# Masking the key-major probabilities of a fused two-layer network on GpSimd instead of adding the mask on TensorE

## The chip, the cores and the metric

The kernel runs on one core of one Trainium2 chip. The metric is the device time of one execution in microseconds (us). Below, PE is TensorE, DVE is VectorE, ACT is ScalarE, POOL is GpSimd and SP is SyncE, which here only issues DMAs.

## What is computed

Sixteen sequences of 512 tokens with 128 features go through two layers: a linear attention and a mixture of experts, then a causal softmax attention and a second mixture of experts. Only the second attention is touched:

```python
B, T, C = x.shape                                   # 16, 512, 128
q = jnp.einsum('btc,oc->bto', x, Wq).reshape(B, T, H, D)   # H 16, D 8
k = jnp.einsum('btc,oc->bto', x, Wk).reshape(B, T, H, D)
v = jnp.einsum('btc,oc->bto', x, Wv).reshape(B, T, H, D)
att = jnp.einsum('bqhd,bkhd->bhqk', q, k) * SCALE
att = jnp.where(mask[None, None, :, :], -jnp.inf, att)     # mask: key j > query i
att = jax.nn.softmax(att, axis=-1)
out = jnp.einsum('bhqk,bkhd->bqhd', att, v).reshape(B, T, C)
```

The mask hides every key behind its query, so of each head's 4 x 4 blocks of 128 the ones below the diagonal are whole, those above are left out by the kernel, and the four on the diagonal are half masked.

## The kernel before

**Stages.** Sequences are pipelined. Each round of the main loop has an x phase and a y phase. The x phase runs the ten expert networks of one sequence on PE, and beside them the scores of another sequence in query-major order, whose row maxima DVE takes (`maxima`). The y phase runs the same scores again in key-major order, 16 heads in 8 pairs, five banks ("fills") a pair, 40 fills a sequence. ACT takes the exponential of each filled bank into `probs` (`exps`, L1014), PE multiplies `probs` by the values (`outputs`, L835), four heads at a time. Beside this, the y phase runs the first attention of a later sequence (`f_...` steps) and the projections q and k of the next one (`r_...` steps). The main loop holds 13 rounds; what comes before and after it is written out.

**Banks and buffers.** Key-major fills go round three PSUM banks `ba0` to `ba2`, so PE may start fill n once ACT has finished fill n-3. `probs` holds three pairs: ACT may write pair p once PE has multiplied pair p-3.

**The mask.** In key-major order the first 128 columns of each head's block of 128 keys are the diagonal block. After each score product (L576) PE adds `mask_k`, zero or -1.0e38, with a second matmul (L578, `identb` as weights): 64 in each sequence, 1024 in all. The query-major scores have their own mask (`mask_q`, L583).

**The chain from q and k to the next x phase.** DVE adds the experts' output to x (L1371), computes the norm (`b_ve`, L1380), centres (`b_n`, L1149), adds a bias to the first attention's projections (`f_bias`, L1180), normalises them (`f_l2` and `f_scale`: 18 small operations at L1193 to L1195 on `rt`, `rn`, and two at L1202), and between them takes the rests of q and k (`qkr`, L1388, once for each). POOL splits each rest in two more parts (`qkp`, L486 and L488). SP writes the parts to device memory (L316), waits until they have landed, and then reads them back in another layout into `QT` and `KT` (L333): 18 transfers for the first eight heads, issued once 20 fills of this y phase are done, and 18 for the others, once all 40 are. The x phase of the next round needs them.

**POOL** also takes reciprocal roots (`power`, L452) and, in the x phase, the products with the gates (`gated`, L459). Its order in the y phase is `power` for `b_rs`, the two splits, `power` for `f_rs`, and the end of the loop.

**The end of a round** is a branch on each engine (L276 on DVE, ACT, PE and POOL). DVE's last work of the y phase are the gates of the experts and the last normalisation (L1404); its first of the x phase is a maximum (L1270).

Of the kernel before, what the change touches and what calls it, by code (L numbers as in the profile page):

```python
# [15 lines left out]
ALU = mybir.AluOpType  # L16
# [3 lines left out]
P = 128  # L20
BATCH, SEQ, D = 16, 512, 128
Q = SEQ // P
TOK = BATCH * SEQ
TILES = TOK // P
HEADS, HD = 16, 8
# [9 lines left out]
MASKED = -1.0e38  # L35
# [10 lines left out]
def build_kernel(nc, a, out):  # L46
    ctx = ExitStack()
    with ctx:
        def sb(name, shape, dt=F32):
            return ctx.enter_context(nc.sbuf_tensor(name, shape, dt))  # L50
# [27 lines left out]
        mask_k = sb("mask_k", [P, P], BF16)  # L78
# [108 lines left out]
        def sb3(name, shape, dt=F32):  # L187
# [56 lines left out]
            s_nmT s_mx0 s_mx1 s_st s_exp s_pv s_oT s_tr s_norm s_aTt s_aT s_wo s_x3 s_y s_ysq s_row s_T4 s_nT4 s_l1 s_l1c  # L244
# [7 lines left out]
        def apart(eng):  # L252

            eng.nop(nofuse=True)
# [164 lines left out]
        def _(pool):  # L419
            c = [1]  # L420

            def const(ins):

                c[0] += 1
                ins.then_inc(S["s_cst"], 1)
                pool.wait_ge(S["s_cst"], c[0])
# [8 lines left out]
            const(pool.memset(mask_k[:], 0.0))  # L435
            const(pool.affine_select(mask_k[:], mask_k[:], [[1, P]], ALU.is_ge, MASKED, base=0, channel_multiplier=-1))
# [40 lines left out]

            def y_phase(b, f, r, t):
                if r is not None:
                    power(b_rs[:], b_ve[:], "s_varb", "s_rsb", r + 1)  # L480
                if r is not None:
                    for w in range(2):

                        pool.wait_ge(S["s_r1"], 2 * r + w + 1)
                        apart(pool)
                        pool.tensor_copy(qkp[:, w, 1], qkr[:, w]).then_inc(S["s_p2"], 1)  # L486
                        pool.wait_ge(S["s_p2"], 2 * r + w + 1)
                        pool.tensor_tensor(qkp[:, w, 2], qkr[:, w], qkp[:, w, 1], ALU.subtract).then_inc(S["s_p3"], 1)  # L488
                if f is not None:
                    power(f_rs[:, 0:Q], f_ve[:, 0:Q], "s_varf", "s_rsf", 2 * f + 2)  # L490
# [67 lines left out]
        def scores(pe, b, n, by_key):  # L558
# [14 lines left out]
            for head, blk, col in groups:  # L573
                if by_key:
                    w = SEQ - blk * P
                    pe.matmul(bank[:, col:col + w], lhsT=KT[0:K_ROWS, head, blk * P:(blk + 1) * P],  # L576
                              rhs=QT[0:K_ROWS, head, blk * P:], start=True, stop=False)
                    last = pe.matmul(bank[:, col:col + P], lhsT=identb[:], rhs=mask_k[:], start=False, stop=True)  # L578
# [19 lines left out]
        def _(pe):  # L598
# [212 lines left out]
            def y_phase(b, f, r, t):  # L811
# [14 lines left out]
                def outputs(k):  # L826
                    pe.wait_ge(S["s_exp"], FILLS * b + 10 * k + 10)
# [820 lines left out]
```

## Time and profile before

| | us |
|---|---|
| median of three runs | 2169.51 |
| lowest and highest | 2169.4, 2172.93 |
| the execution that was profiled | 2157.45 |
| its span, first to last instruction | 2155.7 |

In the profiled span PE is busy for 1617.6 us (75%), DVE 1274.6 (59%), ACT 807.2 (37%) and POOL 510.8 (24%). One round of the main loop takes about 105 us; the loop and the sequences before and after it take up the first 1760 us or so, and the expert lists and the second mixture of experts the rest. Busy shares are means over such stages. The way to read this profile is to take one round, to find in it the waits that end last, and to ask which of them the edited work feeds.

### The profile page before, as it was taken

The page shows a single profiled execution, that of the slowest core. Times are in us where ns is not written, and L with a number is a line of the kernel's source. Part 1 is how long each engine was busy: PE and PEld are TensorE (multiplying, and loading weights), DVE is VectorE, ACT ScalarE, POOL GpSimd, SP SyncE. Part 2 cuts the span into 40 slices and gives each one's busy share as a digit, 9 for nine tenths or more (in the row PEclk, how much of TensorE's full clock was granted, in tenths as well). Part 3 has the DMA queues.
Part 4 walks back from the last instruction along what each step waited for, and adds up shares of the span by engine and source line. Part 5 has one row for each costly group of instructions (what it writes and reads, how often), then busy time and mean ns, then how long its engine had stood idle before and what let it go on. Part 6 is the DMA issues. An engine that isn't in the chain of part 4 may idle for free.

```text
span 2155.7 us, 35078 instructions
## 1 busy us (share of the span) xinstructions
PE 1617.6 (75%) x10136; PEld 908.6 (42%) x10136; DVE 1274.6 (59%) x3878; ACT 807.2 (37%) x1562; POOL 510.8 (24%) x481
## 2 busy tenths in 40 slices
PE   3779888887979797979797979797998831166771
PEld 2345444444444444444444444343544421145551
DVE  5456857575858484848485757576773547721113
ACT  1225252525344443434343435252534322323322
POOL 2321212121202121212121212112120020038884
PEclk7879998999999898989898999998998665588886
DMA  5032240304040403040404031313123000025457
GB/s 143 21 44 42 25 61 10 63 7 68 4 69 7 64 7 64 14 56 15 55 22 48 25 46 30 41 33 38 35 31 56 17 6 0 0 59 99 88 88 170
DMA packets 121515, 95.40 MB, mean 44 GB/s; under 512 B 13120, under 2 KB 115904, under 8 KB 121408
## 3 DMA queue, kind: packets, MB, share of 16 engines
q1 hardware_dynamic: 110144, 85.29, 22.3%
q0 software_dynamic: 11264, 9.05, 3.4%
q14 instruction: 85, 0.70, 0.2%
q8 instruction: 22, 0.36, 0.1%
HBM read 63.34 MB, written 30.18 MB: 43 GB/s over the span
## 4 chain that ended last, share of the span: by engine, by line
PE 38%; issue 26%; DVE 15%; POOL 6%; DMA 6%; ACT 3%; SPq 2%; DVEq 1%; POOLq 0%; ACTq 0%
PE bo L835 5%; PE ba L576 5%; PE fa L665 4%; PE ba L581 4%; PE fa L681 4%; POOL sum_rows L543 3%; PE facc L691 3%; SPq L333 2%; PE ba L578 2%; PE ba L583 2%; DMA xin<-in_L_attn_x 1%; DMA KT<-qk_parts 1%; POOL got L520 1%; DMA sum_rows<-contrib,cur 1%; DVE nm L1270 1%
## 5 line engine op out<-in xcount | busy, mean ns | idle before, releaser
L581 PE MATMUL ba<-KT,QT 72*128 72x512 bf16 (+3 forms) x1024 | 263.2, 320 | 181.1 <-DVE nm L1270 128.5
L1014 ACT ACTIVATE probs<-ba 128x512 f32<-128x512 f32 x640 | 330.2, 622 | 114.1 <-PE ba L578 113.4
L459 POOL TENSOR_TENSOR hh<-th,gb 128x512 f32<-128x512 f32 x128 | 162.1, 1267 | 706.6 <-ACT gb L967 432.7
L1270 DVE TENSOR_REDUCE nm<-ba 128x1 f32<-128x512 f32 x256 | 174.1, 680 | 182.5 <-issue 134.3
L576 PE MATMUL ba<-QT,KT 75*128 75x512 bf16 (+3 forms) x1024 | 252.6, 310 | 34.8 <-ACT probs L1014 28.8
L581 PEld LDWEIGHTS ba<-KT,QT 72*128 72x128 bf16 x1024 | 104.9, 102 | 343.8 <-DVE nm L1270 153.2
L583 PE MATMUL ba<-mask_q,identb 128*128 128x128 bf16 x1024 | 201.3, 230 | 0.0
L578 PE MATMUL ba<-mask_k,identb 128*128 128x128 bf16 x1024 | 195.7, 224 | 0.0
L665 PE MATMUL fa<-f_nT,w 128*128 128x512 f32 x320 | 186.8, 667 | 2.4 <-ACT sc L1048 1.2
L681 PE MATMUL fa<-f_nT,w 128*128 128x512 f32 x320 | 180.0, 645 | 0.0
L983 ACT ACTIVATE sil<-fa 128x512 f32<-128x512 f32 x160 | 95.1, 594 | 217.1 <-PE fa L665 217.0
L967 ACT ACTIVATE gb<-fa 128x512 f32<-128x512 f32 x128 | 76.3, 596 | 256.6 <-PE fa L673 256.5
L691 PE MATMUL facc<-hh,w 128*128 128x512 f32 x320 | 166.2, 602 | 0.0
L576 PEld LDWEIGHTS ba<-QT,KT 75*128 75x128 bf16 x1024 | 102.0, 100 | 148.7 <-ACT probs L1014 93.2
L835 PE MATMUL bo<-probs,vp 128*32 128x512 f32 (+3 forms) x2048 | 154.5, 443 | 0.8 <-DVE ao L1404 0.8
L1272 DVE TENSOR_REDUCE nm<-ba 128x1 f32<-128x384 f32 x256 | 139.9, 546 | 23.2 <-PE ba L583 23.1
L583 PEld LDWEIGHTS ba<-mask_q,identb 128*128 128x128 bf16 x1024 | 106.1, 104 | 82.4 <-issue 80.1
L452 POOL TENSOR_TENSOR b_rs<-b_ve,mhalf 128x4 f32<-128x4 f32 x48 | 48.5, 1010 | 334.3 <-DVE b_ve L1380 227.5
L1395 DVE COPY oT<-bo 128x512 f32<-128x512 f32 x64 | 44.1, 690 | 115.7 <-PE bo L835 114.7
L543 POOL DMA_INDIRECT sum_rows<-contrib,cur x64 | 100.7, 1573 | 30.8 <-issue 18.6
L578 PEld LDWEIGHTS ba<-mask_k,identb 128*128 128x128 bf16 x1024 | 102.8, 100 | 4.6 <-issue 3.7
L835 PEld LDWEIGHTS bo<-probs,vp 128*32 128x32 f32 x2048 | 60.5, 111 | 99.6 <-issue 72.6
(283 smaller groups left out, 2731.7 us busy)
## 6 DMA issues: line engine op xcount, KB each, us to landing
QT<-qk_parts SPq DMA_DIRECT2D x288, 64.0 KB
KT<-qk_parts SPq DMA_DIRECT2D x288, 64.0 KB
qk_parts<-qkp SPq DMA_DIRECT2D x32, 384.0 KB, 2.5
fc<-in_L_ffn_fc_weight SPq DMA_DIRECT2D x32, 256.0 KB, 3.2
xn_rows<-row SPq DMA_DIRECT2D x16, 288.0 KB, 2.5
sum_rows<-zrow SPq DMA_DIRECT2D x1, 4224.0 KB, 22.0
sums<-sum_rows SPq DMA_DIRECT2D x4, 1056.0 KB, 10.4
xin<-in_L_attn_x SPq DMA_DIRECT2D x16, 256.0 KB, 14.0
```

The lines of the kernel that those rows point to most:

```text
L459: pool.tensor_tensor(hh[:, e % 2], th[:, e % 2], gb[:, e % 2], ALU.mult).then_inc(S["s_h"], 1)
L543: pool.indirect_dma_start(sum_rows, bass.IndirectOffsetOnAxis(cur[k][:, c:c + 1], 0), contrib[k % 2][:, c], None, compute_op=ALU.add).then ...
L576: pe.matmul(bank[:, col:col + w], lhsT=KT[0:K_ROWS, head, blk * P:(blk + 1) * P], rhs=QT[0:K_ROWS, head, blk * P:], start=True, stop=False)
L578: last = pe.matmul(bank[:, col:col + P], lhsT=identb[:], rhs=mask_k[:], start=False, stop=True)
L581: pe.matmul(bank[:, col:col + w], lhsT=QT[0:QK_ROWS, head, blk * P:(blk + 1) * P], rhs=KT[0:QK_ROWS, head, 0:w], start=True, stop=False)
L583: last = pe.matmul(bank[:, col + w - P:col + w], lhsT=identb[:], rhs=mask_q[:], start=False, stop=True)
L665: pe.matmul(fa[0][:], lhsT=w1[:, e], rhs=f_nT[:], start=True, stop=True).then_inc(S["s_h1"], 1)
L681: pe.matmul(fa[1][:], lhsT=w3[:, e], rhs=f_nT[:], start=True, stop=True).then_inc(S["s_h3"], 1)
L691: pe.matmul(facc[:], lhsT=w2[:, e], rhs=hh[:, e % 2], start=e == 0, stop=e == U0 - 1).then_inc(S["s_ym"], 1)
L835: last = pe.matmul(bo[32 * j:32 * j + 32, blk * P:], lhsT=vp[:, blk, 4 * k + j], rhs=prob_block(4 * k + j, blk), start=blk == 0, stop=blk ...
L1014: act.activation(probs[:, pair % 3, f_], ba[n % 3][:], ACT.Exp, scale=SCALE).then_inc(S["s_exp"], 1)
L1270: last = dve.tensor_reduce(nm[:, 3, h:h + 1], bank[:], X, ALU.max, negate=True)
```

## The change

The matmul with `mask_k` after each key-major score product goes, with the constant itself. A new function `cut` on POOL waits for each exponential and writes zeros over the masked triangle of its diagonal blocks in `probs`, in place: one `affine_select` a fill, over one block (fills 0 and 2 of a pair) or over two blocks at once (fills 1, 3 and 4). `outputs` on PE waits for the new semaphore `s_cut` instead of `s_exp`. POOL's y phase is written in a new order around the cuts.

```diff
+            def cut(b, pair):
+
+                for f_ in range(5):
+                    pool.wait_ge(S["s_exp"], FILLS * b + 5 * pair + f_ + 1)
+                    apart(pool)
+                    row_ = probs[:, pair % 3, f_]
+                    if f_ in (0, 2):
+                        block_ = row_[:, 0:P]
+                        pool.affine_select(block_, block_, [[1, P]], ALU.is_ge, 0.0, base=0, channel_multiplier=-1).then_inc(S["s_cut"], 1)
+                    else:
+                        apart_by = 384 if f_ < 4 else 256
+                        blocks = row_.rearrange("p (n k) -> p n k", k=P)[:, 0:apart_by // P + 1:apart_by // P]
+                        pool.affine_select(blocks, blocks, [[0, 2], [1, P]], ALU.is_ge, 0.0, base=0, channel_multiplier=-1).then_inc(S["s_cut"], 1)
+
             def y_phase(b, f, r, t):
                 if r is not None:
                     power(b_rs[:], b_ve[:], "s_varb", "s_rsb", r + 1)
-                if r is not None:
-                    for w in range(2):
-
+                for pair in range(HEADS // 2):
+                    if b is not None:
+                        cut(b, pair)
+                    if r is not None and pair in (1, 2):
+                        w = pair - 1
                         pool.wait_ge(S["s_r1"], 2 * r + w + 1)
                         apart(pool)
                         pool.tensor_copy(qkp[:, w, 1], qkr[:, w]).then_inc(S["s_p2"], 1)
                         pool.wait_ge(S["s_p2"], 2 * r + w + 1)
                         pool.tensor_tensor(qkp[:, w, 2], qkr[:, w], qkp[:, w, 1], ALU.subtract).then_inc(S["s_p3"], 1)
-                if f is not None:
-                    power(f_rs[:, 0:Q], f_ve[:, 0:Q], "s_varf", "s_rsf", 2 * f + 2)
+                    if f is not None and pair == 4:
+                        power(f_rs[:, 0:Q], f_ve[:, 0:Q], "s_varf", "s_rsf", 2 * f + 2)
...
-                    pe.matmul(bank[:, col:col + w], lhsT=KT[0:K_ROWS, head, blk * P:(blk + 1) * P],
-                              rhs=QT[0:K_ROWS, head, blk * P:], start=True, stop=False)
-                    last = pe.matmul(bank[:, col:col + P], lhsT=identb[:], rhs=mask_k[:], start=False, stop=True)
+                    last = pe.matmul(bank[:, col:col + w], lhsT=KT[0:K_ROWS, head, blk * P:(blk + 1) * P],
+                                     rhs=QT[0:K_ROWS, head, blk * P:], start=True, stop=True)
...
-                    pe.wait_ge(S["s_exp"], FILLS * b + 10 * k + 10)
+                    pe.wait_ge(S["s_cut"], FILLS * b + 10 * k + 10)
```

POOL in the loop's y phase, before, from the root for `b_rs` to the end of the round (ISA and REGISTER_ALU rows are register work; the semaphores in brackets are those an instruction waits for):

```order
L452 TENSOR_TENSOR b_rs<-b_ve,mhalf 128x4 [waits s_varb]
L484 ISA
L486 CAST qkp<-qkr 128x512 [waits s_r1]
L488 TENSOR_TENSOR qkp<-qkr,qkp 128x512 [waits s_p2]
...
L452 TENSOR_TENSOR f_rs<-f_ve,mhalf 128x4 [waits s_varf]
L276 REGISTER_ALU
L276 COMPARE_AND_BRANCH
```

POOL at the same root for `f_rs`, after: the end of pair 4's cuts, the root, and the beginning of pair 5's:

```order
L487 AFFINE_SELECT probs<-probs 128x2x128 [waits s_exp]
L448 REGISTER_ALU
L449 TENSOR_TENSOR f_rs<-f_ve,mhalf 128x4 [waits s_varf]
L478 REGISTER_ALU
L483 AFFINE_SELECT probs<-probs 128x128 [waits s_exp]
```

So 25 cuts now stand ahead of this root in POOL's order and 15 behind it, and the 15 can't begin before it has run. The splits likewise stand behind the cuts of pairs 1 and 2.

PE before the third `outputs` of the y phase (heads 8 to 11), before:

```order
L576 MATMUL ba<-QT,KT 128x384 [waits s_exp]
L578 MATMUL ba<-mask_k,identb 128x128
L576 MATMUL ba<-QT,KT 128x128
...
L576 MATMUL ba<-QT,KT 128x256 [waits s_exp]
...
L835 MATMUL bo<-probs,vp 32x512 [waits s_norm,s_exp]
L835 MATMUL bo<-probs,vp 32x512 x3
```

PE at the same place, after:

```order
L589 MATMUL ba<-QT,KT 128x384 [waits s_exp]
L589 MATMUL ba<-QT,KT 128x128
L589 MATMUL ba<-QT,KT 128x256 [waits s_exp]
L589 MATMUL ba<-QT,KT 128x256
L847 MATMUL bo<-probs,vp 32x512 [waits s_norm,s_cut]
L847 MATMUL bo<-probs,vp 32x512 x3
```

Every second matmul of the key-major scores is gone, and the first product of each `outputs` now waits for POOL. This third one needs the cuts of pairs 4 and 5, and pair 5's are the first behind the root.

## Rows read from the trace of the kernel before

**Rows 1.** The page: span, and busy time of PE and POOL.

```profile
span 2155.7 us, 35078 instructions
PE 1617.6 (75%) x10136; PEld 908.6 (42%) x10136; DVE 1274.6 (59%) x3878; ACT 807.2 (37%) x1562; POOL 510.8 (24%) x481
```

**Rows 2.** Waits: who waited for whom, total us, times, longest.

```profile
DVE nm L1270 <- issue: 134.3, 12, 12.4
```

**Rows 3.** Chain that ended last, 950 to 1070: start, us, what.

```profile
1021.27 0.66 PE bo L842 x4
...
1048.40 11.01 issue
```

**Rows 4.** Timeline of SP's DMA issues, one round: start, us, line.

```profile
1017.54 5.66 SPq L316 DMA_DIRECT2D qk_parts<-qkp  x2
1025.61 0.32 SPq L333 DMA_DIRECT2D QT<-qk_parts  x1
...
1040.16 0.28 SPq L333 DMA_DIRECT2D QT<-qk_parts  x1
...
1048.72 0.67 SPq L333 DMA_DIRECT2D KT<-qk_parts  x1
```

**Rows 5.** Stretches: us, busy of the five engines, PEclk, DMA share, GB/s.

```profile
1053.00:1059.00 6.00, 0.00 (x0) 0.00 (x0) 0.00 (x0) 0.22 (x1) 0.00 (x0) 0.72 0.59 79
1059.00:1062.00 3.00, 1.73 (x6) 1.05 (x7) 2.48 (x6) 0.00 (x0) 0.00 (x0) 0.50 0.49 80
1062.00:1066.00 4.00, 4.00 (x11) 1.52 (x9) 2.02 (x5) 1.08 (x2) 1.26 (x1) 0.51 0.02 4
```

**Rows 6.** Timeline of DVE in the same round: start, us, line, operation.

```profile
1004.39 0.69 DVE L1371 TENSOR_TENSOR x<-facc,x 128x512 f32 x1 [1.43 <-PE facc L808]
...
1008.26 1.12 DVE L1149 TENSOR_SCALAR b_n<-x,b_mv,b_rs 128x128 f32 x4
...
1014.34 0.40 DVE L1195 SCALAR_TENSOR_TENSOR rn<-rt,rn 128x64 f32<-128x64 f32 x2
...
1016.27 1.27 DVE L1195 SCALAR_TENSOR_TENSOR rn<-rt,rn 128x64 f32<-128x64 f32 x2
...
1018.73 1.29 DVE L1202 TENSOR_TENSOR kvq<-kvq,rn 128x512 f32<-128x512 f32 x2
1019.93 0.68 DVE L1388 TENSOR_TENSOR qkr<-facc,qkp 128x512 f32<-128x512 f32 x1
```

**Rows 7.** Timeline of POOL in the same round.

```profile
1007.22 1.01 POOL L452 TENSOR_TENSOR b_rs<-b_ve,mhalf 128x4 f32<-128x4 f32 x1 [14.73 <-DVE b_ve L1380]
...
1016.16 1.16 POOL L488 TENSOR_TENSOR qkp<-qkr,qkp 128x512 bf16<-128x512 f32 x1
...
1033.92 1.01 POOL L452 TENSOR_TENSOR f_rs<-f_ve,mhalf 128x4 f32<-128x4 f32 x1 [11.31 <-DVE f_ve L1216]
```

**Rows 8.** Groups of POOL instructions by form: count, busy us, mean ns.

```profile
L439 POOL TENSOR_SCALAR_AFFINE_SELECT pick<-pick 128x1024 bf16<-128x1024 bf16 x3 | 3.3, 1091 | 0.4
L436 POOL TENSOR_SCALAR_AFFINE_SELECT mask_k<-mask_k 128x128 bf16<-128x128 bf16 x1 | 0.3, 292 | 0.1
```

**Rows 9.** Timeline of PE: a mask, the product behind it, and the third outputs.

```profile
1024.05 0.22 PE L578 MATMUL ba<-mask_k,identb 128*128 128x128 bf16 x1
1024.11 0.33 PE L576 MATMUL ba<-QT,KT 75*128 75x384 bf16 x1
...
1033.97 2.36 PE L835 MATMUL bo<-probs,vp 128*32 128x512 f32 x32
```

**Rows 10.** Timeline of ACT: exponentials of pairs 0 (three of five), 1, 5 with 6, and 7.

```profile
1006.54 1.57 ACT L1014 ACTIVATE probs<-ba 128x512 f32<-128x512 f32 x3 [0.50 <-PE ba L578]
...
1011.57 2.54 ACT L1014 ACTIVATE probs<-ba 128x512 f32<-128x512 f32 x5
...
1029.94 5.01 ACT L1014 ACTIVATE probs<-ba 128x512 f32<-128x512 f32 x10 [2.70 <-PE ba L578]
...
1038.30 2.55 ACT L1014 ACTIVATE probs<-ba 128x512 f32<-128x512 f32 x5
```

More of the change, by code:

```diff
@@ L77, in build_kernel @@
         mask_q = sb("mask_q", [P, P], BF16)
-        mask_k = sb("mask_k", [P, P], BF16)
         pick = sb("pick", [P, E0, P], BF16)
@@ L243, in build_kernel @@
             s_pad s_lnb s_varb s_rsb s_T3 s_nT3 s_q s_k s_v s_p1 s_r1 s_p2 s_p3 s_vp s_qkw s_qk0 s_qk1 s_S s_red s_nmp s_nmt
-            s_nmT s_mx0 s_mx1 s_st s_exp s_pv s_oT s_tr s_norm s_aTt s_aT s_wo s_x3 s_y s_ysq s_row s_T4 s_nT4 s_l1 s_l1c
+            s_nmT s_mx0 s_mx1 s_st s_exp s_cut s_pv s_oT s_tr s_norm s_aTt s_aT s_wo s_x3 s_y s_ysq s_row s_T4 s_nT4 s_l1 s_l1c
             s_l1x s_ex1 s_prob s_rowd s_mstep s_zero
@@ L434, in _ @@
             const(pool.affine_select(mask_q[:], mask_q[:], [[-1, P]], ALU.is_ge, MASKED, base=0, channel_multiplier=1))
-            const(pool.memset(mask_k[:], 0.0))
-            const(pool.affine_select(mask_k[:], mask_k[:], [[1, P]], ALU.is_ge, MASKED, base=0, channel_multiplier=-1))
             const(pool.memset(pick[:], 0.0))
```

## The prediction

> **What bounds the kernel now.** The page shows PE busy for 75% of the span [rows 1]. That would make any matmul taken out look like a gain, so I read next what ends the waits inside one round of the loop.
>
> The list of waits has one odd entry: DVE sits for 134.3 us in 12 waits in front of its first maximum of the x phase, 11.2 us each, and no engine or DMA is named for them, only "issue" [rows 2]. The loop has 13 rounds and returns 12 times, so this is what a return to the loop's head costs. The chain of waits has the same piece: 11.01 us from 1048.40 [rows 3]. Meanwhile PE, DVE and POOL do nothing at all, and the DMA engines stay at a share near 0.59 until about 1061.5; then their share falls to 0.02 [rows 5]. I read this as DVE's instructions at the loop's head being fetched by DMA, behind the queue of QT and KT transfers. The Trainium skill says, in "Runtime: NRT & Kernel Launch", section "Instruction fetch mechanics", that a taken branch out of the window of pages at hand must fetch the page by DMA before going on; the rows agree in kind, and the length (11 us) is this case's own.
>
> So one round is tied to its transfers. SP issues the first of the 36 at 1025.61 and the last at 1048.72 [rows 4], and they drain at about 1061.5, some 36 us after the first. The first waits for q and k to be split and written: the second rest starts on DVE at 1019.93 [rows 6], 5.7 us before it. And that rest is reached by a DVE chain of 15.5 us from 1004.39 (the experts' output added) which has hardly an idle moment [rows 6]. **The y phase's first half is DVE's, its end is hidden behind a DMA queue, and PE's load is in neither.** At the chain's end PE's turn of the first outputs starts at 1021.27, right behind DVE's work on the second rest and one copy of its outputs [rows 3, 6], so the rest of the y phase follows DVE too.
>
> **What is taken out.** A mask takes PE 0.06 us: one starts at 1024.05 and the next product at 1024.11 [rows 9] (the 0.22 us shown is the length of its pipeline). At 0.057 us, 64 masks are 3.6 us a sequence. ACT's ten exponentials back to back take 5.01 us [rows 10], so where ACT sets the pace the gain hides. Ahead of 1021 DVE sets it. What is left is PE's dense stretch from 1021 to 1030 and the first fills of some pairs, some 20 masks: 1.2 us, at the end of the y phase. Ends: 0 and 3.6.
>
> **What is added on POOL.** An affine_select of 128 columns took 292 ns and one of 1024 columns 1091 ns [rows 8], so by the line between them one of 256 takes 0.406. A pair has two of the first and three of the second: 1.80 us of work, 14.4 a sequence, beside ACT's 2.55 us for a pair's five exponentials [rows 10]. POOL keeps up with ACT and trails by about one cut, 0.4 to 0.5 us. For outputs 1, 2 and 4 PE arrives later than that or nearly so: I take 0.
>
> **What the cuts do to DVE: the first main term.** Two operations at L1195 take 0.40 us alone (1014.34) and 1.27 at 1016.27, where POOL's subtraction runs from 1016.16 to 1017.32 [rows 6, 7]: DVE is held until POOL is through. L1195 reads two SBUF tensors, and so do L1193, L1194 and L1202. The Trainium skill has the rule in "SBUF — State Buffer", section "Who interferes with whom": a DVE instruction with two SBUF inputs, or in a 2-port mode, and a GpSimd instruction that reads SBUF exclude each other for the whole of it. It speaks against this change; by it alone the term would be the upper end below. From the rows, by pair:
> - Pair 0: the first three exponentials are done by 1008.11 [rows 10] and the root at 1008.23 [rows 7]; three cuts (0.29 + 0.41 + 0.29 = 0.99 us) fall on the four centrings at 1008.26 [rows 6], which PE, ACT's square and DVE itself wait for. I take 0.8.
> - Pair 1: its exponentials run from 1011.57 to 1014.11 [rows 10], and its last three cuts (1.1 us) fall on the small operations that end at 1014.74 [rows 6]. Short operations slip into the gaps between cuts: 0.7.
> - Pair 2: POOL does the first split at the same time as before, so all five cuts (1.8 us) start at about 1017.4 and fall on the last six small operations and on L1202 (1018.73, 1.29 for both) [rows 6]: 1.4.
>
> Together 2.9 us a round later to the second rest, the transfers and all behind. Ends: 0, if cuts don't hold DVE, and 3.9 (0.99 + 1.1 + 1.8). I choose nearer the upper, since the held row is of the same two engines and operands.
>
> **The root for f_rs: the second main term.** It stood alone; now 15 cuts stand behind it, and it can't start before DVE's variance, at 1033.92 [rows 7]. It ends at 1034.93. Then pair 5 is cut: 1.80 us and five gaps of 0.07, so 1037.1. PE's third outputs started at 1033.97 [rows 9] and needs these cuts: 3.1 us of new wait. POOL's cuts and DVE's centring after the root also hold each other (1.1 us at most): 3.1 to 4.2, and I take 3.1. Queued behind it on PE are the last pair's scores, so ACT's last exponentials, DVE's gates and the branch. The y phase thus ends 3.1 - 1.2 = 1.9 us later than the first term alone makes it.
>
> **How much of that the loop's return hides.** If the wait at the branch ends with the drain, 1.9 us cost nothing; if it always lasts 11 us, they cost 1.9. The branch comes 23 us behind the first transfer of 36, so the queue is a third full and gets shorter; I take half, 0.9.
>
> **The sum.** A round with a return costs 2.9 + 0.9 = 3.8 us, times 12: 45.6. The y phases of sequences 0 and 13 have no return behind them: 2.9 + 1.9 = 4.8 each, 9.6. The last two have no first attention beside them, so neither L1193 to L1202 nor the root: gain and delay about even, 0. In all +55 us. On the profiled span 2155.7 that makes 2211. The profiled execution (2157.45) is 12 us under the median of the runs (2169.51); on the median the forecast is 2169.5 + 55 = **2225**.
>
> **Rivals.**
> - **Cuts don't hold DVE.** For it: no affine_select runs beside DVE work in this trace. Against: the row at 1016.27. Only the root's term remains: 12 x 0.9 + 2 x 1.9 = 15 us: 2184. Chance 0.15.
> - **All at its upper end.** DVE held for all of each cut (3.9), centring and cuts holding each other (4.2 - 1.2 = 3.0), and the return's wait as long as ever: 6.9 x 14 = 97: 2266. For it: the return's 12 waits vary little (mean 11.2, longest 12.4). Also, the granted clock is 0.5, 1.2 GHz, for PE after the idle of the return [rows 5], and a PE waiting 3 us at the third outputs might meet this too. Chance 0.17.
> - **No difference.** Cuts don't hold DVE and the drain takes in the root's delay: 2 x 1.9 = 4 us: 2173. Chance 0.06.
> - **Faster, because PE's time counts.** If cuts cost DVE nothing, and the return's wait is not the transfers' but of a fixed length behind a branch that PE brings forward, each y phase ends earlier by what PE gains. It decides once more masks lie on the path than the 3.1 us of the root: 55 of the 64 in each. With all 64 and the root's wait hidden, 16 x 3.6 = 58 us less: 2111; with 1.2 us a sequence, 2150. Against it: ACT's and DVE's paces above. Chance 0.07.
>
> The forecast has 0.55. For an 80% range I leave out the faster cases and the far end of the upper one: 2176 to 2272. About 0.2% (4 us) is what a measurement of this kernel can tell. Faster 0.07, within 0.2% 0.06, slower 0.87.
>
> **What the profile of the changed kernel would show.** L1193 to L1195 and L1202 taking longer on average than 0.2 and 0.69 us each; DVE from L1371 to the second rest 18.4 us instead of 15.5; first transfer still 5.7 us behind the rest; PE waiting about 3 us for POOL's cut ahead of the third outputs; DVE's wait at the loop's return shorter, near 10 us; a round near 109 us instead of 105. I am wrong if DVE's chain keeps its 15.5 us, if the cut waits show ahead of other outputs, or if the x phase starts earlier after the transfers than 34 us.

## The result, and the profile after

| | before | changed |
|---|---|---|
| median of the runs, us | 2169.45 (4 runs) | 2254.74 (4 runs) |
| lowest and highest | 2167.32, 2172.93 | 2233.04, 2262.35 |
| profiled execution | 2157.45 | 2262.35 |

The changed kernel takes 1.0375 times as long (95% interval 1.0303 to 1.0448): 85 us more where the forecast said 55 more. In the profiled executions 93 of the 105 us between the two spans lie in the 12 full rounds of the loop: 112.6 us a round on average instead of 104.8. So the question is where 7.8 us a round come from. These two executions lie 20 us further apart than the medians do (the one before is 12 us under its median, the changed one 8 over), so 7.8 us is what the two traces show and rather more than the usual round loses.

The page of the changed kernel, span and engines, to be read against [rows 1]:

```profile
span 2260.3 us, 34827 instructions
PE 1633.3 (72%) x9112; PEld 859.8 (38%) x9112; DVE 1292.9 (57%) x3878; ACT 804.2 (36%) x1562; POOL 728.8 (32%) x1119
```

PE has 1024 matmuls fewer and is busy for 16 us more. The costliest groups say which matmuls grew (busy us, mean ns of one | idle just before them, and for whom). First before, then after:

```profile
L835 PE MATMUL bo<-probs,vp 128*32 128x512 f32 (+3 forms) x2048 | 154.5, 443 | 0.8 <-DVE ao L1404 0.8
```

```profile
L847 PE MATMUL bo<-probs,vp 128*32 128x512 f32 (+3 forms) x2048 | 206.6, 559 | 36.3 <-POOL probs L487 36.3
...
L487 POOL TENSOR_SCALAR_AFFINE_SELECT probs<-probs 128x256 f32<-128x256 f32 x384 | 155.3, 411 | 36.5 <-ACT probs L1026 30.6
...
L483 POOL TENSOR_SCALAR_AFFINE_SELECT probs<-probs 128x128 f32<-128x128 f32 x256 | 74.5, 291 | 151.6 <-ACT probs L1026 146.6
```

The same 2048 output matmuls take 52 us more of PE's time and wait 36.3 us for POOL, in 16 waits. The cuts cost what the line between [rows 8] said (292 and 406 ns): 291 and 411 ns.

**DVE's chain.** DVE in one round, which starts at 1179.67 as [rows 6] starts at 1004.39:

```profile
1179.67 0.69 DVE L1383 TENSOR_TENSOR x<-facc,x 128x512 f32 x1 [1.43 <-PE facc L820]
...
1183.54 1.20 DVE L1161 TENSOR_SCALAR b_n<-x,b_mv,b_rs 128x128 f32 x4
...
1190.04 0.41 DVE L1207 SCALAR_TENSOR_TENSOR rn<-rt,rn 128x64 f32<-128x64 f32 x2
...
1191.97 1.38 DVE L1207 SCALAR_TENSOR_TENSOR rn<-rt,rn 128x64 f32<-128x64 f32 x2
1193.28 0.68 DVE L1205 SCALAR_TENSOR_TENSOR rt<-n,rn 128x64 f32<-128x64 f32 x2
1193.88 0.80 DVE L1206 TENSOR_TENSOR rt<-rt,rn 128x64 f32<-128x64 f32 x2
...
1195.12 1.29 DVE L1214 TENSOR_TENSOR kvq<-kvq,rn 128x512 f32<-128x512 f32 x2
1196.33 0.68 DVE L1400 TENSOR_TENSOR qkr<-facc,qkp 128x512 f32<-128x512 f32 x1
```

From the first to the last row are 16.7 us, before 15.5. The centrings beside three cuts take 1.20 us instead of 1.12, two pairs of small operations beside pair 2's cuts 0.68 and 0.80 instead of 0.40 and 0.41, and L1214 has kept its 1.29: the five cuts of pair 2 lay beside small operations for their whole length, and were over when L1214 began. The rest is POOL in the same round, with the cuts of pair 2 and, behind the root, those of pairs 5 and 6:

```profile
1191.88 1.15 POOL L501 TENSOR_TENSOR qkp<-qkr,qkp 128x512 bf16<-128x512 f32 x1
1192.98 0.29 POOL L483 TENSOR_SCALAR_AFFINE_SELECT probs<-probs 128x128 f32<-128x128 f32 x1
1193.23 0.41 POOL L487 TENSOR_SCALAR_AFFINE_SELECT probs<-probs 128x256 f32<-128x256 f32 x1
1193.59 0.29 POOL L483 TENSOR_SCALAR_AFFINE_SELECT probs<-probs 128x128 f32<-128x128 f32 x1
1193.84 0.77 POOL L487 TENSOR_SCALAR_AFFINE_SELECT probs<-probs 128x256 f32<-128x256 f32 x2
...
1209.66 1.01 POOL L449 TENSOR_TENSOR f_rs<-f_ve,mhalf 128x4 f32<-128x4 f32 x1 [5.95 <-DVE f_ve L1228]
...
1211.52 0.76 POOL L487 TENSOR_SCALAR_AFFINE_SELECT probs<-probs 128x256 f32<-128x256 f32 x2
```

The five cuts last 1.63 us from 1192.98, less than the sum of their own times, since they overlap.

**The third outputs and the clock.** PE in the same round: fills of pairs 5 and 6, the third outputs, and the fourth:

```profile
1206.52 3.33 PE L589 MATMUL ba<-QT,KT 75*128 75x384 bf16 x12
1212.34 4.50 PE L847 MATMUL bo<-probs,vp 128*32 128x512 f32 x32 [2.49 <-POOL probs L487]
...
1224.08 2.83 PE L847 MATMUL bo<-probs,vp 128*32 128x512 f32 x32
```

The third outputs start 32.7 us behind the round's beginning; before, 29.6 (1033.97 less 1004.39) [rows 6, 9]. That is 3.1 us later, and 2.49 us of it are PE's wait for POOL. Then they take 4.50 us where they took 2.36. The stretches say why (us, busy of PE, PEld, DVE, ACT, POOL, granted clock as a share of full speed, DMA share, GB/s), after:

```profile
1209.00:1212.00 3.00, 0.75 (x4) 0.19 (x4) 1.77 (x9) 1.87 (x4) 2.34 (x6) 0.90 0.57 56
1212.00:1218.00 6.00, 5.67 (x36) 2.01 (x37) 0.69 (x2) 0.00 (x0) 1.86 (x6) 0.50 0.58 59
1218.00:1222.00 4.00, 2.73 (x21) 2.18 (x19) 0.55 (x2) 3.05 (x6) 1.45 (x5) 0.93 0.58 60
1222.00:1225.00 3.00, 3.00 (x18) 2.12 (x21) 2.24 (x13) 0.23 (x1) 0.35 (x1) 0.50 0.58 60
```

and before, from the third outputs on:

```profile
1034.00:1037.00 3.00, 3.00 (x40) 1.45 (x40) 1.72 (x5) 0.95 (x2) 0.92 (x1) 1.00 0.59 59
1037.00:1043.00 6.00, 4.82 (x44) 3.51 (x45) 1.94 (x11) 3.27 (x7) 0.00 (x0) 1.00 0.58 64
```

While PE waits for the cuts the granted clock falls to 0.50, that is 1.2 GHz instead of 2.4, and the 32 matmuls behind the wait, and all else on PE for 6 us, run at half speed; in this round it falls once more at 1222. In every one of the 12 rounds of this execution such a drop begins 30 to 32 us behind the round's beginning and lasts 6.8 us; in eight of them a second one follows. Taken over the stretch from 29 to 44 us behind that point, the clock is 0.66 to 0.77 in all of them; before it was 1.00 in 11 and 0.89 in one.

**The transfers and the return.** SP in the same round: first and last of the first half, of the second:

```profile
1202.02 0.32 SPq L332 DMA_DIRECT2D QT<-qk_parts  x1
...
1208.77 0.28 SPq L332 DMA_DIRECT2D KT<-qk_parts  x1
...
1221.01 0.28 SPq L332 DMA_DIRECT2D QT<-qk_parts  x1
...
1227.92 0.28 SPq L332 DMA_DIRECT2D KT<-qk_parts  x1
```

The first is still 5.7 us behind the rest of 1196.33. The second half comes 19.0 us behind it (18.3 to 19.0 in all rounds), before 14.5 [rows 4], for it waits until all 40 fills are done, and these wait for the root and run at the low clock. The wait at the return, to be read against [rows 2], and its last row on DVE in this round:

```profile
DVE nm L1282 <- issue: 142.9, 12, 13.8
```

```profile
1243.73 0.69 DVE L1282 TENSOR_REDUCE nm<-ba 128x1 f32<-128x512 f32 x1 [12.75 <-issue]
```

It has grown, from 11.2 to 11.9 us on average, though it now begins 26.8 to 30.7 us behind the first transfer instead of 23. It hides nothing of the delay.

### The profile page after: what moved, and what is told of

The parts are those of the page before. It is cut to its first block, busy times and chain, and to the rows that moved or that the text cites. A ratio compares the mean times of both kernels' runs of the same rounds, so it can differ in the third digit from the quotient of the medians.

```text
span 2260.3 us, 34827 instructions
## 1 busy us (share of the span) xinstructions
PE 1633.3 (72%) x9112; PEld 859.8 (38%) x9112; DVE 1292.9 (57%) x3878; ACT 804.2 (36%) x1562; POOL 728.8 (32%) x1119
## 4 chain that ended last, share of the span: by engine, by line
PE 35%; issue 27%; DVE 14%; POOL 7%; ACT 6%; DMA 4%; SPq 2%; DVEq 1%; ACTq 0%; POOLq 0%
PE bo L847 8%; ACT probs L1026 4%; PE fa L677 4%; PE fa L693 4%; PE ba L593 3%; POOL sum_rows L556 3%; PE facc L703 3%; PE ba L589 2%; SPq L332 2%; POOL got L533 1%; DMA xin<-in_L_attn_x 1%; PE ba L595 1%; DVE nm L1282 1%; PE fa L685 1%; DVE passed L1484 1%
## 5 line engine op out<-in xcount | busy, mean ns | idle before, releaser
L589 PE MATMUL ba<-QT,KT 75*128 75x512 bf16 (+3 forms) x1024 | 221.0, 316 | 57.9 <-ACT probs L1026 34.9
L593 PEld LDWEIGHTS ba<-KT,QT 72*128 72x128 bf16 x1024 | 104.6, 102 | 355.7 <-DVE nm L1282 171.4
L847 PE MATMUL bo<-probs,vp 128*32 128x512 f32 (+3 forms) x2048 | 206.6, 559 | 36.3 <-POOL probs L487 36.3
L487 POOL TENSOR_SCALAR_AFFINE_SELECT probs<-probs 128x256 f32<-128x256 f32 x384 | 155.3, 411 | 36.5 <-ACT probs L1026 30.6
L1407 DVE COPY oT<-bo 128x512 f32<-128x512 f32 x64 | 44.2, 690 | 195.5 <-PE bo L847 195.2
L589 PEld LDWEIGHTS ba<-QT,KT 75*128 75x128 bf16 x1024 | 77.5, 99 | 193.1 <-ACT probs L1026 141.3
L847 PEld LDWEIGHTS bo<-probs,vp 128*32 128x32 f32 x2048 | 71.1, 134 | 181.7 <-issue 132.3
L483 POOL TENSOR_SCALAR_AFFINE_SELECT probs<-probs 128x128 f32<-128x128 f32 x256 | 74.5, 291 | 151.6 <-ACT probs L1026 146.6
```

What stands on the lines that cost most here:

```text
L487: pool.affine_select(blocks, blocks, [[0, 2], [1, P]], ALU.is_ge, 0.0, base=0, channel_multiplier=-1).then_inc(S["s_cut"], 1)
L589: last = pe.matmul(bank[:, col:col + w], lhsT=KT[0:K_ROWS, head, blk * P:(blk + 1) * P], rhs=QT[0:K_ROWS, head, blk * P:], start=True, sto ...
L593: pe.matmul(bank[:, col:col + w], lhsT=QT[0:QK_ROWS, head, blk * P:(blk + 1) * P], rhs=KT[0:QK_ROWS, head, 0:w], start=True, stop=False)
L847: last = pe.matmul(bo[32 * j:32 * j + 32, blk * P:], lhsT=vp[:, blk, 4 * k + j], rhs=prob_block(4 * k + j, blk), start=blk == 0, stop=blk ...
```

## The experiments

All time ratios are against the kernel before on the same chip, where its median was 2163.75 us beside r1 to r4, 2165.27 beside r5 to r8 and 2164.35 beside r9 to r11. "Clean" rounds are those with a granted clock of 0.93 or more from 29 to 44 us behind the round's beginning. The per-round numbers are worked out from the trace of each profiled execution, over 12 rounds. "To the return" is the time from a round's beginning to DVE's wait at the loop's return, over the clean rounds (over all 12). It is the finer measure: in the clean rounds before it lies between 44.1 and 44.5 us, while the whole round scatters from 102.5 to 106.1, mostly by the return's wait (9.6 to 12.4 us) and the x phase. A difference of 1 us between two means of whole rounds is hardly more than this scatter.

| kernel | median (range), us | ratio | chain, us | to the return, us | clean rounds | other rounds |
|---|---|---|---|---|---|---|
| before | 2169.45 | 1 | 15.5 | 44.2 (44.4) | 11 of 104.6 us | 1 of 107.8 |
| changed | 2254.74 | 1.0375 | 16.7 | none (51.4) | none | 12 of 112.6 |
| r1_root_after_5 | 2185.13 (2178.07 to 2194.74) | 1.0107 | 16.7 | 44.3 (46.0) | 7 of 105.6 | 5 of 108.7 |
| r2_no_mask | 2176.75 (2169.65 to 2190.82) | 1.0057 | 15.5 | 43.4 (45.8) | 4 of 104.3 | 8 of 107.7 |
| r3_masks_and_cuts | 2250.00 (2239.91 to 2262.22) | 1.0405 | 16.7 | none (50.0) | none | 12 of 111.9 |
| r4_filler | 2232.49 (2226.58 to 2235.01) | 1.0323 | 16.7 | 46.9 (48.6) | 6 of 107.8 | 6 of 111.8 |
| r7_masks_cuts_after_5 | 2188.37 (2174.86 to 2194.3) | 1.0106 | 16.7 | 45.7 (46.2) | 7 of 106.0 | 5 of 107.5 |
| r8_cut2_later | 2176.14 (2161.73 to 2192.88) | 1.0068 | 16.0 | 43.8 (45.3) | 8 of 104.8 | 4 of 108.6 |
| r6_write_only | 2206.51 (one run) | | 15.5 | none (48.7) | none | 12 of 108.8 |
| r5_late_half | 2059.08 (2049.06 to 2062.07) | 0.9495 | 15.5 | 44.3 (44.4) | 11 of 96.2 | 1 of 97.3 |
| r9_late_changed | 2154.34 (2142.15 to 2167.06) | 0.9965 | 16.7 | none (51.7) | none | 12 of 103.7 |
| r10_late_cut2 | 2072.54 (2051.91 to 2076.66) | 0.9591 | 16.0 | 43.8 (44.6) | 8 of 96.0 | 4 of 98.3 |
| r11_late_no_mask | 2065.29 (2048.88 to 2071.97) | 0.9530 | 15.5 | 43.3 (45.0) | 7 of 95.5 | 5 of 99.9 |

**The root behind pair 5's cuts (r1_root_after_5).** The root's wait is taken away, all else stays.

```diff
-                    if f is not None and pair == 4:
+                    if f is not None and pair == 5:
```

> The changed kernel with one thing moved: the root for f_rs stands behind pair 5's cuts instead of pair 4's, so the third outputs no longer wait for it. Theory A (of the 8 us that a round gained, the root's place is the most: 3.1 us of wait ahead of the third outputs, and behind it PE at a granted clock of 0.5, which stretches those outputs from 2.36 to 4.50 us): no wait for POOL ahead of the third outputs, these at 2.4 us, a round near 106 us, total 2175 to 2195. Theory B (the cuts themselves cost, by holding DVE and by trailing ACT): rounds stay near 112 us, total above 2230. The share of the cuts holding DVE (1.2 us a round in the chain up to the second rest, 16.7 instead of 15.5) stays in either.

Of the 85 us some 62 are gone. One index in POOL's order was worth nearly three quarters of the loss. In the clean rounds DVE is at the return after 44.3 us, against 44.2 before: the chain's 1.1 us more are made up by the masks that are gone (r2 has their price). What is left comes mostly from the other five rounds, in which the clock falls here too, though PE waits for nothing ahead of its third outputs:

```profile
1366.74 4.05 PE L847 MATMUL bo<-probs,vp 128*32 128x512 f32 x32
```

So the wait for the cuts brings the drop in every round, but it isn't the only thing that can.

**No masks, no cuts (r2_no_mask).** What is PE's gain worth by itself?

```diff
-                    pe.matmul(bank[:, col:col + w], lhsT=KT[0:K_ROWS, head, blk * P:(blk + 1) * P],
-                              rhs=QT[0:K_ROWS, head, blk * P:], start=True, stop=False)
-                    last = pe.matmul(bank[:, col:col + P], lhsT=identb[:], rhs=mask_k[:], start=False, stop=True)
+                    last = pe.matmul(bank[:, col:col + w], lhsT=KT[0:K_ROWS, head, blk * P:(blk + 1) * P],
+                              rhs=QT[0:K_ROWS, head, blk * P:], start=True, stop=True)
```

> The kernel before without the key-major masks and without any cuts: the masked triangle is left out of the computation altogether, so this is the price of the 64 matmuls alone. Theory A (a round is tied to DVE's chain, the transfers and the return, and PE's 3.6 us lie beside them): 0 to 1.2 us a round less, total 2150 to 2170. The rival (PE's time counts): 3.6 us a sequence less, 2111.

Missed: it is slower than the kernel with the masks, by 0.3 to 0.8%, with the chain as before and no wait added. At full clock the masks are worth something: in the two rounds with a clock of 1.00 DVE is at the return after 43.2 us instead of 44.2, 1.0 us of the 3.6. But only these two keep the clock at 1.00 from 29 to 44 us; two have 0.93, and in the other eight it is 0.68 to 0.89, and DVE is at the return after 47.0 us on average. Stretches of one of the eight and of one of the two with 0.93, at the same points of their rounds:

```profile
1054.00:1058.00 4.00, 2.87 (x36) 1.42 (x28) 1.81 (x5) 1.50 (x4) 0.19 (x1) 1.00 0.58 65
1058.00:1062.00 4.00, 3.86 (x21) 3.57 (x22) 1.12 (x5) 2.06 (x5) 0.00 (x0) 0.62 0.58 66
1062.00:1066.00 4.00, 4.00 (x25) 1.63 (x28) 2.18 (x12) 0.12 (x1) 0.00 (x0) 0.52 0.58 69
```

```profile
1269.00:1273.00 4.00, 2.82 (x36) 1.42 (x29) 1.81 (x5) 1.50 (x4) 0.15 (x1) 1.00 0.58 62
1273.00:1277.00 4.00, 3.90 (x36) 2.89 (x40) 1.92 (x11) 2.14 (x5) 0.00 (x0) 1.00 0.58 63
1277.00:1281.00 4.00, 2.06 (x32) 0.99 (x24) 3.89 (x19) 0.60 (x1) 0.00 (x0) 0.98 0.58 67
```

PE does the same in both first rows; the first of the two rounds loses its clock right behind, at 1059, the second keeps it until 1281. The drop follows a wait of 1.18 us for ACT, here in the round that lost it:

```profile
1058.04 0.88 PE L576 MATMUL ba<-QT,KT 75*128 75x384 bf16 x4 [1.18 <-ACT probs L1013]
```

The kernel before has this wait too, at the same point, and keeps the clock; with its masks PE was busy for 3.73 us of the four, not 2.8 to 2.9:

```profile
1139.00:1143.00 4.00, 3.73 (x44) 1.83 (x44) 1.81 (x5) 1.14 (x3) 0.88 (x1) 1.00 0.59 62
```

What decides between two rounds that look alike stays open.

**Masks and cuts (r3_masks_and_cuts).** The changed kernel with the mask matmuls put back.

```diff
+        mask_k = sb("mask_k", [P, P], BF16)
...
-                    last = pe.matmul(bank[:, col:col + w], lhsT=KT[0:K_ROWS, head, blk * P:(blk + 1) * P],
-                                     rhs=QT[0:K_ROWS, head, blk * P:], start=True, stop=True)
+                    pe.matmul(bank[:, col:col + w], lhsT=KT[0:K_ROWS, head, blk * P:(blk + 1) * P],
+                              rhs=QT[0:K_ROWS, head, blk * P:], start=True, stop=False)
+                    last = pe.matmul(bank[:, col:col + P], lhsT=identb[:], rhs=mask_k[:], start=False, stop=True)
```

> The changed kernel with the mask matmuls kept as well (POOL's cuts in the same order, outputs waiting for them): the masks' price in the presence of the cuts. Theory A: within 1.2 us a round of the changed kernel, 2250 to 2275; if the masks keep PE's clock up, even equal. The rival (PE's time counts once PE is late): 3.6 x 16 = 58 us above it, 2313.

It equals the changed kernel within the intervals, with 1024 matmuls more. The clock stays a little higher (0.77 to 0.89) and PE does more: that evens out. So the masks save next to nothing here, and the cuts carry the loss.

**PE kept busy through the wait (r4_filler).** Eleven matmuls that no one reads stand ahead of the third outputs, in front of the wait for the cuts.

```diff
-                    pe.wait_ge(S["s_cut"], FILLS * b + 10 * k + 10)
...
+                    if k == 2:
+                        for _ in range(11):
+                            pe.matmul(bo[:], lhsT=identb[:], rhs=pick[:, 0:4], start=True, stop=True)
+                    pe.wait_ge(S["s_cut"], FILLS * b + 10 * k + 10)
```

> The changed kernel with 11 matmuls of 512 bf16 columns (0.22 us each, 2.4 us in all) on PE ahead of the third outputs, where it waits for POOL; they write a bank that the outputs then overwrite. Theory A holds the drop of the granted clock to 0.5 for 3 to 4 us of the 8 us a round: with PE busy in the wait the clock stays at 1.0, third outputs take 2.4 us again, a round is 2 to 4 us shorter, total 2200 to 2225. If the clock is only a companion of the wait and hidden behind the transfers, no change: 2245 to 2262.

Half a hit: the time lies 7 us above the range. The third outputs behind the fillers take their old 2.36 us in all 12 rounds. Six rounds keep the full clock, as this one:

```profile
1196.45 2.32 PE L845 MATMUL bo<-pick,identb 128*128 128x512 bf16 x10
1198.88 2.36 PE L850 MATMUL bo<-probs,vp 128*32 128x512 f32 x32
```

In the other six the clock falls nevertheless, in five of them while the fillers run, which are then slow themselves:

```profile
1303.61 4.01 PE L845 MATMUL bo<-pick,identb 128*128 128x512 bf16 x10
1307.55 2.36 PE L850 MATMUL bo<-probs,vp 128*32 128x512 f32 x32
```

In the clean rounds DVE is at the return after 46.9 us: at full clock the root's wait costs 2.5 us over the 44.3 of r1_root_after_5. The changed kernel takes 51.4, and these further 4.5 us go with the clock.

**Masks, cuts, root late (r7_masks_cuts_after_5)**: the edits of r1 and r3 together.

```diff
-                    if f is not None and pair == 4:
+                    if f is not None and pair == 5:
...
+                    pe.matmul(bank[:, col:col + w], lhsT=KT[0:K_ROWS, head, blk * P:(blk + 1) * P],
+                              rhs=QT[0:K_ROWS, head, blk * P:], start=True, stop=False)
+                    last = pe.matmul(bank[:, col:col + P], lhsT=identb[:], rhs=mask_k[:], start=False, stop=True)
```

> The mask matmuls and the cuts together, with the root for f_rs behind pair 5's cuts. Against the same kernel without the masks (r1_root_after_5, 2185) it adds 64 matmuls of 0.06 us to a sequence. Theory A now (the masks keep PE busy between ACT's releases, and without them the granted clock falls to 0.5 in some rounds, which costs 4 to 6 us in each): all rounds keep the clock at 1.0 up to the branch, a round is 105 to 106.5 us, total 2172 to 2185, so no slower than without the masks although it does more. The rival (PE's work costs its time): 1.2 to 3.6 us a sequence more than r1_root_after_5, 2204 to 2243.

The time lies 3 us above the range, and not all rounds keep the full clock: it is 1.00 in seven and 0.89 in five, where without masks it is 0.66 to 0.68 in three. The time is that of r1_root_after_5. With r2 and r3 this is the third pair in which PE's 3.6 us of masks a round are worth nothing in the total: what they cost at full clock (45.7 us to the return against 44.3 here) they give back in clock (46.2 against 46.0 over all rounds).

**Pair 2's cuts behind the second split (r8_cut2_later)**, on top of r1.

```diff
-                    if b is not None:
+                    if b is not None and pair != 2:
+                        cut(b, pair)
+                    if b is not None and r is None and pair == 2:
                         cut(b, pair)
...
                         pool.tensor_tensor(qkp[:, w, 2], qkr[:, w], qkp[:, w, 1], ALU.subtract).then_inc(S["s_p3"], 1)
+                        if b is not None and pair == 2:
+                            cut(b, pair)
```

> The kernel r1_root_after_5 with pair 2's five cuts moved behind the second split. Theory A (these cuts fall on DVE's operations with two SBUF inputs): the chain up to the second rest falls from 16.7 us to 15.9 to 16.1; the second outputs must not start later than POOL's cuts of pairs 2 and 3, which then end about 20 to 22.5 us behind the experts' output added, as they do. Total 0 to 12 us under r1_root_after_5, if the clock's drops come as often. The rival (the hold comes from pairs 0 and 1): chain at 16.7.

The chain takes 16.0 us: pair 2's cuts cost 0.7, those of pairs 0 and 1 the other 0.4.

**Writing without reading (r6_write_only).** Each cut is a fill with ones over the same block, which reads nothing from SBUF.

```diff
-                        pool.affine_select(block_, block_, [[1, P]], ALU.is_ge, 0.0, base=0, channel_multiplier=-1).then_inc(S["s_cut"], 1)
+                        pool.memset(block_, 1.0).then_inc(S["s_cut"], 1)
...
-                        pool.affine_select(blocks, blocks, [[0, 2], [1, P]], ALU.is_ge, 0.0, base=0, channel_multiplier=-1).then_inc(S["s_cut"], 1)
+                        pool.memset(blocks, 1.0).then_inc(S["s_cut"], 1)
```

> The changed kernel in which each affine_select is a memset over the same blocks: POOL writes in the same places and order but reads nothing (the diagonal blocks' values are left out of the computation, ones stand there). Theory A (DVE's operations with two SBUF inputs are held while POOL reads SBUF): the chain from the experts' output added to the second rest of q and k falls from 16.7 us back to 15.5. The rival (any POOL instruction holds DVE): it stays above 16.2. The total stays near that of the changed kernel, 2235 to 2262, since the root's place and PE's clock are as there.

One run: 2206.51. The chain takes 15.5 us in all rounds (from 1141.97 to 1157.52 here), and the small operations beside the fills are back at 0.40:

```profile
1155.09 0.41 DVE L1205 SCALAR_TENSOR_TENSOR rt<-n,rn 128x64 f32<-128x64 f32 x2
1155.45 0.40 DVE L1206 TENSOR_TENSOR rt<-rt,rn 128x64 f32<-128x64 f32 x2
```

while POOL fills beside them:

```profile
1154.99 0.31 POOL L487 MEMSET probs<- 128x256 f32 x1
1155.24 0.20 POOL L483 MEMSET probs<- 128x128 f32 x1
```

So it is POOL's reading that holds these two-input operations. The Trainium skill says just this in "SBUF — State Buffer", section "Who interferes with whom": such a DVE instruction contends with a GpSimd instruction that reads SBUF, not with one that only writes. The total lies 28 us under the range, which had taken no account of the fills being shorter (207 and 311 ns): the waits at the outputs are 28.2 us in 16 instead of 36.3, and the clock is 0.89 in five rounds.

**The second half of the transfers behind the return (r5_late_half).** The kernel before; SP issues the second 18 transfers once DVE has taken its first maximum of the x phase. It asks whether the return's wait is the transfers'.

```diff
-            def back_dmas(b, half):
+            def back_dmas(b, half, late=False):
+                if late:
+                    sp.wait_ge(S["s_red"], FILLS * b + 1)
+                    apart(sp)
...
                 load_x(i + 2)
+                back_dmas(i, 1, late=True)
                 both(max_dmas, i)
                 row_dmas(i - 1)
                 part_dmas(i + 1)
-                both(back_dmas, i + 1)
+                back_dmas(i + 1, 0)
...
+            back_dmas(n - 1, 1, late=True)
```

> The kernel before with one thing moved: inside the loop the 18 transfers for the second eight heads are issued after DVE's first maximum of the x phase, so that they are not queued when DVE returns to the loop's head. Theory A (the 11 us at the return are a fetch of instructions behind those transfers): the wait falls from 11.2 us to under 4 us in each of 12 returns; x phase's second half may wait a few us for its heads, so a round is 3 to 8 us shorter and the total 2080 to 2130. The rival (the return has a length of its own): the wait stays at 10 to 12 us and the total at 2165 or above.

It is, by more than expected (the time lies 21 us under the range), and this is the fastest kernel of the case: 5% less than before. Its wait at the return:

```profile
DVE nm L1275 <- issue: 33.4, 12, 3.0
```

```profile
q14 instruction: 1, 0.01, 12.2%
```

In the 12 returns before, the first such packet starts 7.2 to 9.7 us behind the beginning of DVE's wait, in r5_late_half 0.8 to 1.1 us, and DVE goes on 2 to 3 us behind it in both. So what the queued transfers lengthen is the time until the instructions are fetched. The second half now arrives beside the x phase's first work, where PE waits 37.4 us for it in all, in 21 waits.

**The change without the return's wait (r9_late_changed), and its relatives (r10_late_cut2, r11_late_no_mask)**: the edit of r5 on the changed kernel, on r8 and on r2. The prediction let the return hide part of the delay; here it can't.

> The changed kernel with the second half of the QT and KT transfers issued behind DVE's first maximum of the x phase, as in r5_late_half, which took 2059.1 us without the cuts. Theory: what the cuts cost is (a) 1.2 us of DVE in the chain to the second rest, (b) about 2 to 3 us of waiting at the third outputs, and (c) a lower granted clock from there on, each of them a cost of the y phase and independent of the return. Then the chain takes 16.7 us, the clock 29 to 44 us behind x2add is under 0.8 in nearly all rounds, the rounds take 103 to 105 us instead of 95.6 to 97, and the time is 2155 to 2180. Rival: the clock is lowered only together with the idle time of the return (15 us in which PE does nothing), which r5_late_half cuts to a third. Then the clock is 0.95 or more in nearly all rounds, the rounds take 99 to 101 us, and the time is 2105 to 2130. In both the return's wait is 3 to 4 us.

> r8_cut2_later (cuts, the root for f_rs behind pair 5's cuts, pair 2's cuts behind the second split) with the late second half of the transfers. r8_cut2_later was 11 us over the kernel before, of which 0.5 us a round is the chain and the rest rounds at a lower clock. Theory: with the return's wait gone, it costs 0.5 to 1 us a round over r5_late_half's 2059.1: 2065 to 2080, chain 16.0. Rival: without masks PE now gets ahead in the y phase, and as the return no longer hides it, the gain of 1.2 us a round shows: 2040 to 2058.

> The kernel before without the key-major masks (the masked triangle is left out of the computation, nothing stands in its place) and with the late second half of the transfers. It asks what the 64 masks a sequence are worth on PE where the return hides nothing. Theory from r2_no_mask (12 us slower than with masks, 7 of 13 rounds at a granted clock of 0.77): PE's spare time is no gain, and the clock falls in some rounds: 2058 to 2075. Rival: the masks were worth 1.2 us a sequence at full clock, and the clock holds: 2040 to 2050.

All three came out by the theory, the time of r9 0.7 us under its lower edge. The changed kernel loses 95 us against r5_late_half, as it loses 85 against the kernel before, and 7.4 us a round; the wait at the return (32.7 us in 12) doesn't matter to it. The third outputs and the clock in one of its rounds:

```profile
935.88 4.50 PE L852 MATMUL bo<-probs,vp 128*32 128x512 f32 x32 [2.48 <-POOL probs L492]
```

```profile
936.00:939.00 3.00, 3.00 (x20) 0.80 (x24) 0.00 (x0) 0.00 (x0) 1.40 (x5) 0.50 0.61 65
```

So the clock's fall belongs to the y phase and its own wait, not to the idle time at the return. Removing the masks pays no better here: the clean rounds are at the return after 43.3 us instead of 44.3 and take 95.5 us against 96.2, and five rounds at a lower clock give it back (the ratios, 0.953 and 0.9495, lie within each other's intervals). No form of the change beats r5_late_half's 2059.08.

## Why the prediction was right, and where not

The time lies inside the range and the direction was right, with the two mechanisms named. That it came so near is in part luck, as the steps show. In us a round:

| step | predicted | measured |
|---|---|---|
| cuts hold DVE | 2.9 | 1.1 |
| root ahead of pair 5's cuts, at full clock | 3.1 | 2.5 |
| PE's gain, at full clock | 1.2 less | 1.0 less |
| clock | nothing in the forecast; named without a price in a rival | 4.5 |
| return | hides 1.0 of 1.9 | hides nothing, and its wait is 0.7 longer |
| sum of a round | 3.8 | 7.8 |

The measured column is worked out from the times to the return: 43.2 us without masks at full clock (r2), 44.2 before, 44.3 with cuts (r1), 46.9 with the root's wait filled (r4), 51.4 in the changed kernel. The 7.8 us are those of the two profiled executions; by the medians a round loses rather less. The 0.7 us at the return is hardly more than that wait's scatter. The two y phases without a return behind them, taken with the x phase that follows, became 4.0 and 5.1 us longer, where the prediction had 4.8 for each.

- **The mis-sized term is the clock.** The prediction saw the 0.5 behind the return in [rows 5], and wrote that a PE waiting 3 us at the third outputs might meet this too, but only in the rival of upper ends, and without a price of its own. It could have been given one: at half the clock the 32 output matmuls take about twice their 2.36 us [rows 9], and all else behind them slows as well. Measured are 4.50 us, and a clock that stays down for 6.8. What the runs show of the cause: the changed kernel has no clean round, r4 with the wait filled has 6, r1 without the wait has 7. So the wait brings a drop in every round (r3 and r9 have no clean round either); the missing masks let the clock fall in some without it (r2 has 4 clean rounds, against 11 before).
- **DVE's hold was over-sized,** for three reasons. The cuts overlap, so that five last 1.63 us and not 1.8. The four centrings, for which the prediction put 0.8, read one tensor from SBUF and grew by 0.08 (1.20 instead of 1.12). And the cuts fell on few of the operations with two: pair 2's cost 0.7 and not 1.4, since they ended before L1214 began, and pairs 0 and 1 together 0.4 and not 1.5. The row it rested on, 1.27 us beside POOL's subtraction, showed one long operation of POOL, and the cuts are many short ones with gaps. By the rule of the Trainium skill which the prediction weighed ("SBUF — State Buffer", section "Who interferes with whom"), the upper end (3.9) would have followed; the trace agrees with it in kind (r6) and not in size.
- **The root's wait was right in its place and too long by 0.5 us.** POOL's root came 0.5 us later in the round than before (30.0 us behind its beginning instead of 29.5), and the five cuts behind it took 0.5 us less than the 2.2 that the prediction reckoned. These two cancel, so that the third outputs start 3.1 us later, the very number of the prediction, which had meant it on top of the 2.9 of the first term.
- **The return.** The prediction reckoned with a queue that starts where it did and so drains where it did. The second half of the transfers is itself released by the y phase's last fills, 4 us later now behind the first transfer, and the drain comes about 21 us behind that release, before and after. So the delay passes through in full. The row that would have shown it is in [rows 4]: the second half starts at 1040.16, behind the waits in question.
- **PE's gain** was taken at 1.2 of 3.6 and is 1.0 at full clock; in the total it is below nothing, since rounds without masks lose clock (r2).
- Of what the profile was to show, the first transfer 5.7 us behind the rest, a wait for POOL ahead of the third outputs (2.5 us for about 3) and longer small operations at L1193 and L1194 were there; L1202's two kept their length, and DVE's chain of 18.4 (16.7), a return wait near 10 (11.9) and a round near 109 (112.6) were not. That the total came near rests on errors of opposite sign: 1.8 too much for DVE and 0.6 for the root, 4.5 too little for the clock and 1.7 for the return. The median of 2254.74 is nearer to the 2266 of the rival of upper ends than to the forecast's 2225, though not by that rival's terms: DVE wasn't held for all of each cut.

## What to carry to other kernels

When work is moved from a busy engine to an idle one, look first at what else stands in the idle engine's order: here one root ahead of 15 cuts, itself waiting for DVE, made nearly three quarters of the loss. A new wait on PE costs its own length and can cost, as here in every round, the time in which PE runs at half clock behind it; price both, the second from rows that show PE's work at either clock. And matmuls taken out of a stretch that another engine paces are little gain (1.0 us of 3.6 a round at full clock, and less than nothing with the clock that went with them); follow instead the wait that nothing is named for, as the 11 us at the loop's return: issuing half of the transfers 12 us later was worth 5%.

## What the runs showed of the hardware

- **Less work on PE can cost time.** With 64 matmuls a sequence taken out and nothing put in, the kernel was 0.57% slower (0.3 to 0.84%, 10 runs): the granted clock, at 2.4 GHz from 29 to 44 us behind the beginning of 11 of 12 rounds before, was at 1.2 GHz for part of this stretch in ten of twelve.
- **Code fetched at a taken branch queues behind data.** DVE's wait was 11.2 us with 36 transfers issued in the 23 us before the branch, and 2.8 us with 18; the first instruction packet started on average 8.4 us behind the beginning of that wait in the one case, and 0.8 in the other. The Trainium skill ("Runtime: NRT & Kernel Launch", section "Instruction fetch mechanics") states that a taken branch out of the pages at hand must fetch its page by DMA before it goes on; the trace agrees, with one packet on the instruction queue in each of these waits.
- **A fill on POOL can hold a DVE operation with one tensor input.** In r6 the four centrings of `f_n`, issued together with the fills behind the root, took 2.72 us; beside cuts, which read and write, they took 1.30, and before, beside nothing, 1.11:

```profile
1145.84 1.11 DVE L1161 TENSOR_SCALAR b_n<-x,b_mv,b_rs 128x128 f32 x4
...
1171.88 2.72 DVE L1161 TENSOR_SCALAR f_n<-x,f_mv,f_rs 128x128 f32<-128x128 f32 x4 [1.12 <-POOL f_rs L449]
```

 The centrings of `b_n`, beside fills as well, keep their 1.11 us (the first row). Why the one is held and the other is not wasn't tried.
